# Attention's two score passes in 64-row tiles of the matmul array (one transformer layer, one core)

## The chip, the cores and the metric

One Trainium2 chip, one of its cores. The metric is the device time of one execution in microseconds (us); smaller is better. Engines are named as in the profile: PE (TensorE, matrix multiply; PEld is its weight load), DVE (VectorE), ACT (ScalarE), POOL (GpSimd), SP (SyncE, here the issuer of all DMAs).

## The reference, cut to what matters

Eight images of 1024 tokens, 128 channels. Everything is float32.

```python
h = x @ W + pos                                      # 29 features -> 128
h = h + attn(layernorm(h))                           # 8 heads of 16 channels, causal
h = h + ffn(layernorm(h))                            # shared swiglu + 8 experts, 2 of them per token
# attn:
scores = einsum('bhqd,bhkd->bhqk', Q, K)
attn = softmax((scores + mask) / math.sqrt(d), axis=-1)
out = einsum('bhqk,bhkd->bhqd', attn, V) @ Wo + bo
```

## The kernel before, in words

**Precision by stacking.** A head has only 16 channels. To keep float32 precision with the fast one-pass matmul type, Q and K are each split into a high and a low part, and three products (high x high, high x low, low x high) are stacked along the contraction rows: 3 x 16 = 48 rows. `k_stack` holds, for each of four head pairs, the even head's 48 rows from row 0 and the odd head's 48 rows from row 64. `q_stack` has a slot per head: an even head's rows are 0 to 47 and the rest of its slot is zero, an odd head's rows are 64 to 111 and rows 0 to 63 are zero. So one matmul over all rows picks the right head of the pair. The zeros are written once, at the start (`stacks_zeroed`: two memsets on DVE, one on POOL).

**Two score passes.** Pass 1 (`score`, line 494; 64 steps per image) computes scores with queries on the output partitions, rows 0 to 111 of the array; DVE adds the mask and takes the row maximum (`score`, line 747). A step of 128 queries has up to 1024 keys, so half the steps are one matmul and half are two: 96 matmuls of 256, 384 or 512 columns per image. Every 16 steps (a unit: four heads, half an image) `turn` transposes the maxima on PE (line 507), DVE splits them (lines 735, 737), and SP copies them as two rows (126 and 127) into `q_stack` (`maxima`, line 375: two DMAs per unit). Against them `k_stack` holds rows of -1. Pass 2 (`prob`, line 523; 96 matmuls per image) computes the scores again, keys on the output partitions, over all 128 rows, so that the maximum is already subtracted; ACT takes the exponential (line 975); `weigh` (line 542, 24 per image) multiplies with V: four heads side by side in four 32-column tiles of the array, as two halves of float32 each, 8 records. Both passes write two alternating buffers (banks `b4`, `b5` for `prob` and the narrow scores, `pair[0]`, `pair[1]` for the wide scores). Step p of `prob` waits for the exponential of step p - 2, and step s of `score` for the maximum of step s - 2.

**The order.** Each engine runs one list of stages, `PERIOD`, woven by hand from streams: s = pass 1, p = pass 2, w = weigh, m = the layer's middle and the next image's front (emb, turn1, q, k, v, and to, ant, oproj, z2t, gates, shared), f = the two matmul layers of the ffn (`in`, `expert`), c = combine. PE takes its list strictly in this order:

```python
WEAVE = (
    "ssppspspspsppswspsppsppwsppsppwsppspwpwsppsppwsspspwppsppspspwpspwpspsppwspspwpssppwppssppwppsps"
    "ppwppmpspwppmwppmppwppmppppwwppmwppmppmwppfpmfppfwpmpmmfpwpmfppfffppmwppfppmpwppppmwsswsswssmssf"
    "mcssfssmfcmfffmssfcmcmfmmssffsfmmfsfsmmfsffssfssfmssfssmccssfsfsfsfscc"
)
```

In a period pass 1 begins with the wide steps (score 32 to 63), and the narrow steps (0 to 31) of the next image end it. `FIRST` goes before the first period, `LAST_WEAVE` is the order of the last image. Six middle images run in a hardware loop.

**The stretches** of one period, in PE's order, from one stage to the next: A from score 32 to the first `to`; B from there to `k` of half 0; C to score 0; D to `emb` of half 1; E to `turn1` of half 1; F to `k` of half 1; G to the end. The stack copies of the next image's K and Q (`stacks`, line 367: twelve DMAs of 128 KB in row behind `k` of half 0) must land before score 0.

**Tiles of the array.** An instruction uses a tile of the array that covers its rows and columns. `weigh` is 128 rows x 32 columns; `emb` (line 437, 29 rows) and the bias matmul inside `shared` (line 644, 9 rows) are 32-row tiles; everything else is the whole 128 x 128.

Of the kernel before, what the change touches and what calls it, by code (L numbers as in the profile page):

```python
# [36 lines left out]
P = 128  # L37
# [5 lines left out]
G4 = 4  # L43
# [5 lines left out]


ODD = 64
STACK = ODD + 3 * DH
SHIFT = P - 2
EPS = 1e-5
MASK = -100000.0
VW = 32
# [108 lines left out]
def build(nc, x_t, tok_w, pos, wq, wk, wv, wo, bq, bk, bv, bo, ln_s, ln_b, w_in, w_shared, w_expert, w_bias,  # L165
          w_gate, b_gate, out):
    with ExitStack() as ctx:
# [3 lines left out]
        def sem(name):  # L171
            return ctx.enter_context(nc.semaphore(name))
# [36 lines left out]
        qk_h, qk_l = sb("qk_h", [P, 2, S], F32R), sb("qk_l", [P, 2, S], F32R)  # L209
        v = sb("v", [P, TILES, HEADS, VW])  # L210

        q_stack = sb("q_stack", [P, 2, HEADS, HALF], F32R)
        k_stack = sb("k_stack", [P, HEADS // 2, S], F32R)
        mx = sb("mx", [P, NS])
        mrow_h, mrow_l = sb("mrow_h", [UNIT_S, NU, P], F32R), sb("mrow_l", [UNIT_S, NU, P], F32R)
# [86 lines left out]
            sem(n) for n in ("ex_ready", "sela_made", "sel_made", "weighted", "ex_step"))  # L302
        out_done = [sem(f"out_done_{half}") for half in range(2)]
        zeroed, ident_made = sem("zeroed"), sem("ident_made")
        stacks_zeroed = sem("stacks_zeroed")
        went_on = sem("went_on")

        out_v = out.rearrange("b (t p) c -> b p t c", p=P)
# [28 lines left out]
        @block.sync  # L337
        def _(sp):
            def load_x(i):
                sp.dma_start(x_sb[:], x_t[:, bass.ds(i * S, S)]).then_inc(x_in, 16)  # L340

            load_x(0)
            for dst, src in ((tokw_sb, tok_w), (pos_sb, pos)):
                sp.dma_start(dst[:], src).then_inc(w_in0, 16)
            for dst, src in ((wq_sb, wq), (wk_sb, wk), (bq_sb, bq), (bk_sb, bk),
                             (wv_sb, wv), (bv_sb, bv), (bo_sb, bo)):
                sp.dma_start(dst[:], src).then_inc(w_in1, 16)
            for dst, src in ((wo_sb, wo), (lns_sb, ln_s), (lnb_sb, ln_b), (win_sb, w_in), (wshared_sb, w_shared),
                             (wex_sb, w_expert), (wbias_sb, w_bias), (wgate_sb, w_gate), (bgate_sb, b_gate)):
                sp.dma_start(dst if dst is win_sb or dst is wex_sb else dst[:], src).then_inc(w_in2, 16)  # L350

            sp.wait_ge(const_made, CONSTS)
            sp.wait_ge(stacks_zeroed, 3)
            for n in range(HEADS // 2):
                sp.dma_start(words(k_stack[SHIFT:P, n, :]), words(minus1.rearrange("r c n -> r (c n)"))).then_inc(ones_in, 16)

            def stacks(i, half, w):

                if w == 0:
                    sp.wait_ge(qkh_made, i * 4 + 2 * half + 2)  # L360
                    sp.wait_ge(qkl_made, i * 4 + 2 * half + 2)
                for n, part in enumerate((qk_h, (qk_h, qk_l)[w], (qk_l, qk_h)[w])):
                    for odd in range(2):
                        to = slice(odd * ODD + n * DH, odd * ODD + (n + 1) * DH)
                        stack = k_stack[to, :, halfs(half)] if w else q_stack[to, half, odd::2, :]
                        rows = part[odd * (P // 2):(odd + 1) * (P // 2), w, halfs(half)]
                        sp.dma_start(words(stack), words(rows)).then_inc(stack_in[half], 16)  # L367

            def maxima(i, u):

                g, half = UNITS[u]
                sp.wait_ge(ml_made, i * NU + u + 1)
                for row, part in ((SHIFT, mrow_h), (SHIFT + 1, mrow_l)):
                    dst = q_stack[row:row + 1, half, g * G4:(g + 1) * G4, :]
                    sp.dma_start(words(dst), words(part[:, u, :])).then_inc(m_in[u], 16)

            def store(i, half):
                sp.wait_ge(ex_step, (i * TILES + (half + 1) * HT) * COMBINE)
                sp.dma_start(out_v[i, :, tiles(half), :], acc[:, tiles(half), :]).then_inc(out_done[half], 16)

            def stage(i, st, loads=True):
                if st[0] == "turn":
                    maxima(i, st[1])
                elif st == ("k", 0):
                    stacks(i, 0, 0)
                    if not later(i):
                        stacks(i, 0, 1)
                elif st == ("k", 1):
                    stacks(i, 1, 0)
                    stacks(i, 1, 1)  # L390
                    if loads:
                        load_x(i + 1)
                elif st == ("combine", 3):
                    store(i, 0)
                elif st == ("combine", 7):
                    store(i, 1)

            def keys(i):

                sp.wait_ge(exp_done, i * NP_ * G4 + (KEYS_USED + 1) * G4)  # L400
                stacks(i + 1, 0, 1)

            def image(i, loads):
                for n, st in enumerate(PERIOD):
                    stage(i + of_next_image(st), st, loads)
                    if n == max(PERIOD.index(("k", 0)), PERIOD.index(("prob", KEYS_USED, G4 - 1))):
                        keys(i)

            for st in FIRST:
                stage(0, st)  # L410
            image(0, True)
            with sp.Fori(1, B - 2) as i:
                image(i, True)
            image(B - 2, False)
            for st in LAST:
                stage(B - 1, st)
            for half in range(2):
                sp.wait_ge(out_done[half], B * 16)
# [3 lines left out]
        def _(pe):  # L422
# [50 lines left out]
            def score(i, s):  # L473


                u, t, j = SCORE_STEPS[s]
                hd = UNITS[u][0] * G4 + j
                if s == 0:
                    pe.wait_ge(stack_in[0], i * 192 + 192)
                    if later(i):  # L480
                        pe.wait_ge(exp_done, i * NP_ * G4)
                if s == UNIT_S:
                    pe.wait_ge(ml_made, i * NU + 1)
                if s == 2 * UNIT_S:
                    pe.wait_ge(stack_in[1], i * 192 + 192)
                    if later(i):
                        pe.wait_ge(sel_made, i * TILES)
                if s >= 2:
                    pe.wait_ge(s_taken, i * NS + s - 1)
                n = (t + 1) * P  # L490
                dst = pair[s % 2] if t >= HT else (b4, b5)[s % 2]

                for a, b in ([(0, max(256, n))] if n <= HALF else [(0, HALF), (HALF, max(HALF + 256, n))]):
                    mm = nc.tensor.matmul(dst[:, a:b], q_stack[0:STACK, t // HT, hd, t % HT * P:(t % HT + 1) * P],  # L494
                                          k_stack[0:STACK, hd // 2, a:b], start=True, stop=True)
                mm.then_inc(s_ready, 1)

            def turn(i, u):
# [11 lines left out]
            def prob(i, k, j):  # L510

                u, kt = PROB_STEPS[k]
                g, half = UNITS[u]
                q0, c0 = prob_columns(k)
                if kt == 0 and j == 0:
                    pe.wait_ge(m_in[u], i * 32 + 32)
                if k == 0 and j == 0:
                    pe.wait_ge(ml_made, i * NU + 2)
                p = k * G4 + j
                if p >= 2:  # L520
                    pe.wait_ge(exp_done, i * NP_ * G4 + p - 1)
                hd = g * G4 + j
                nc.tensor.matmul((b4, b5)[p % 2][:, c0:HALF], k_stack[:, hd // 2, kt * P:(kt + 1) * P],  # L523
                                 q_stack[:, half, hd, c0:HALF], start=True, stop=True).then_inc(st_ready, 1)

            def weigh(i, k):

# [165 lines left out]
            pe.wait_ge(wsplit_qk, 4)  # L693
            for st in FIRST[1:]:
                stage(0, st)
            pe.wait_ge(ones_in, HEADS // 2 * 16)
            pe.wait_ge(w_in2, 9 * 16)
            pe.wait_ge(wsplit_h, 2)
            pe.wait_ge(wsplit_l, 2)
# [8 lines left out]
        def _(dve):  # L708
# [31 lines left out]
            def score(i, s):  # L740
                u, t, j = SCORE_STEPS[s]
                n = (t + 1) * P
                col = u * UNIT_S + j * HT + t % HT
                alone(dve, s_ready, i * NS + s + 1)
                src = (pair[s % 2] if t >= HT else (b4, b5)[s % 2])[:, 0:n]

                nc.vector.tensor_tensor_reduce(src, src, causal[:, S - n:S], 1.0, -3.0e38, ALU.add, ALU.max,  # L747
                                               mx[:, col:col + 1]).then_inc(s_taken, 1)
# [168 lines left out]
                for st in PERIOD:  # L917
                    stage(i + of_next_image(st), st)

            nc.vector.memset(words(k_stack[:, 0:2, :]), 0.0).then_inc(stacks_zeroed, 1)  # L920
            dve.wait_ge(w_in0, 2 * 16)
            stage(0, FIRST[0])
            dve.wait_ge(w_in1, 7 * 16)
# [4 lines left out]
                nc.vector.tensor_tensor(wqk_l[:, n, :], w[:], wqk_h[:, n, :].bitcast(F32),  # L928
                                        ALU.subtract).then_inc(wsplit_qk, 1)
            stage(0, FIRST[1])  # L930
            nc.vector.memset(words(k_stack[:, 2:, :]), 0.0).then_inc(stacks_zeroed, 1)
            dve.wait_ge(const_made, CONSTS)
            for st in FIRST[2:]:
                stage(0, st)
# [131 lines left out]
        def _(pool):  # L1066
# [2 lines left out]
            pool.wait_ge(zeroed, 1)  # L1069
            nc.gpsimd.affine_select(out=ident[:], in_=ident[:], compare_op=ALU.not_equal, fill=1.0, base=0,  # L1070
                                    pattern=[[-1, P]], channel_multiplier=1).then_inc(ident_made, 1)
            nc.gpsimd.memset(words(q_stack[:]), 0.0).then_inc(stacks_zeroed, 1)
            pool.wait_ge(const_made, 1)

            def constants():
# [171 lines left out]
```

## Time and profile before

| | us |
|---|---|
| time before, median of 3 runs (lowest, highest) | 1200.93 (1200.56, 1201.93) |
| span of the profiled execution, first to last instruction | 1198.4 |
| the median less this span (start and end around the program) | 2.5 |
| PE busy in the span | 1062.6 |
| DVE, ACT, POOL busy | 760.6, 629.2, 388.1 |

The profiled execution's time is its span with what lies around it; no time of its own is listed beside the three runs. A middle image takes 143.5 us. A matmul's busy time in the profile is its latency: it overlaps with the next one's, so the distance between two starts, not the duration, tells what an instruction costs PE.

### The profile page before, as it was taken

How to read it: one execution, taken by the hardware profiler on the slowest of the kernel's cores; microseconds unless marked ns; L12 is line 12 of the kernel's file. 1: busy time of each engine (PE TensorE's matmuls, PEld its weight loads, DVE VectorE, ACT ScalarE, POOL GpSimd, SP SyncE). 2: the span in 40 equal slices, each digit the busy share in tenths (PEclk: the TensorE clock that was granted, in tenths of full speed). 3: DMA queues.
4: the chain of work that ended last, by engine and by line, in shares of the span. 5: the costliest groups of instructions: out<-in, count | busy, mean ns of one | idle time of the engine just before them, and what ended most of it. 6: DMA issues, size and time to landing. Idle time of an engine off the chain costs nothing.

```text
span 1198.4 us, 20365 instructions
## 1 busy us (share of the span) xinstructions
PE 1062.6 (89%) x5632; PEld 707.3 (59%) x5632; DVE 760.6 (63%) x2118; ACT 629.2 (52%) x1395; POOL 388.1 (32%) x514
## 2 busy tenths in 40 slices
PE   2579988999799988899888998889989899899997
PEld 1345566556675566655666556755567455675575
DVE  3378547873768547686486854777467763778444
ACT  1226825567345745467344672546734576456744
POOL 5411424314341234313352142431433213341133
PEclk9969989999898998899889998989988999899999
DMA  3430033004040040400413003310314004040000
GB/s 94 71 40 2 14 41 59 19 2 54 10 59 10 1 53 10 67 1 1 53 26 50 1 11 42 55 22 1 41 12 66 13 2 53 10 63 1 1 2 18
DMA packets 28540, 34.39 MB, mean 29 GB/s; under 512 B 5402, under 2 KB 15552, under 8 KB 28336
## 3 DMA queue, kind: packets, MB, share of 16 engines
q1 hardware_dynamic: 28464, 33.55, 18.2%
q8 instruction: 26, 0.43, 0.1%
q14 instruction: 50, 0.41, 0.1%
HBM read 3.61 MB, written 4.19 MB: 7 GB/s over the span
## 4 chain that ended last, share of the span: by engine, by line
PE 62%; issue 11%; DVE 8%; DMA 6%; POOL 5%; SPq 4%; ACT 3%; DVEq 0%; POOLq 0%; ACTq 0%
PE bank L523 12%; PE pair L494 10%; PE bank L542 9%; PE bank L494 5%; DMA k_stack<-qk_h 5%; SPq L367 4%; PE pair L662 4%; PE pair L663 4%; PE pair L664 4%; PE bank L643 2%; ACT pt L975 2%; PE pair L425 1%; PE pair L426 1%; PE pair L427 1%; PE bank L644 1%
## 5 line engine op out<-in xcount | busy, mean ns | idle before, releaser
L975 ACT ACTIVATE pt<-bank 128x512 f32<-128x512 f32 (+3 forms) x768 | 348.6, 494 | 230.8 <-PE bank L523 223.6
L747 DVE CUSTOM_DVE_ANT_0 pair<-pair,causal 128x640 f32<-128x640 f32 (+3 forms) x256 | 258.8, 1046 | 59.3 <-PE pair L494 44.8
L523 PE MATMUL bank<-q_stack,k_stack 128*128 128x512 f32 (+2 forms) x768 | 268.9, 402 | 7.8 <-ACT pt L975 6.3
L523 PEld LDWEIGHTS bank<-q_stack,k_stack 128*128 128x128 f32 x768 | 137.9, 193 | 160.2 <-ACT pt L975 127.6
L1119 POOL TENSOR_SCALAR_AFFINE_SELECT pt<-pt 128x512 f32<-128x512 f32 x128 | 81.6, 638 | 391.9 <-ACT pt L975 391.9
L494 PE MATMUL pair<-k_stack,q_stack 112*128 112x512 f32 (+2 forms) x512 | 156.2, 396 | 22.6 <-DVE mx L747 12.3
L747 DVE CUSTOM_DVE_ANT_0 bank<-bank,causal 128x128 f32<-128x128 f32 (+3 forms) x256 | 122.6, 507 | 73.3 <-PE bank L494 73.1
L542 PE MATMUL bank<-pt,v 128*32 128x512 f32 (+3 forms) x1536 | 165.5, 503 | 2.2 <-POOL pt L1119 1.8
L494 PEld LDWEIGHTS pair<-k_stack,q_stack 112*128 112x128 f32 x512 | 90.9, 202 | 62.4 <-DVE mx L747 42.3
L494 PE MATMUL bank<-k_stack,q_stack 112*128 112x256 f32 (+2 forms) x256 | 90.0, 424 | 33.2 <-DMA k_stack<-qk_h 23.8
L662 PE MATMUL pair<-wex_h,hid_h 128*128 128x512 f32 x256 | 106.3, 415 | 0.7 <-POOL hid_l L1142 0.4
L663 PE MATMUL pair<-wex_l,hid_h 128*128 128x512 f32 x256 | 103.7, 405 | 0.0
L1021 ACT ACTIVATE from_act<-pair,gm 128x512 f32<-128x512 f32 x64 | 44.1, 689 | 113.3 <-PE pair L664 105.5
L664 PE MATMUL pair<-wex_h,hid_l 128*128 128x512 f32 x256 | 103.2, 403 | 0.0
L1150 POOL TENSOR_TENSOR from_dve<-from_act 128x256 f32<-128x256 f32 x64 | 46.7, 729 | 171.9 <-ACT from_act L1027 171.2
L1027 ACT ACTIVATE from_act<-from_dve,wsel 128x128 f32<-128x128 f32 x256 | 81.7, 391 | 37.6 <-DVE from_dve L899 37.6
L494 PEld LDWEIGHTS bank<-k_stack,q_stack 112*128 112x128 f32 x256 | 52.7, 227 | 54.5 <-DVE mx L747 20.0
L899 DVE SCALAR_TENSOR_TENSOR from_dve<-pair,gm,from_act 128x512 f32<-128x512 f32 x64 | 47.8, 746 | 41.8 <-PE pair L664 30.2
L747 DVE DVE_READ_ACCUMULATOR2_ANT mx<- 128x1 f32 x512 | 72.4, 141 | 0.1
L872 DVE SCALAR_TENSOR_TENSOR from_dve<-from_act,pair 128x512 f32<-128x512 f32 x64 | 43.9, 686 | 43.6 <-PE pair L427 33.3
L425 PE MATMUL pair<-z2t_h,win_h 128*128 128x512 f32 x128 | 58.1, 454 | 2.6 <-issue 1.8
L664 PEld LDWEIGHTS pair<-wex_h,hid_l 128*128 128x128 f32 x256 | 49.7, 194 | 12.4
(142 smaller groups left out, 1528.7 us busy)
## 6 DMA issues: line engine op xcount, KB each, us to landing
q_stack<-qk_h SPq DMA_DIRECT2D x64, 128.0 KB, 4.1
k_stack<-qk_h SPq DMA_DIRECT2D x64, 128.0 KB, 6.2
q_stack<-qk_l SPq DMA_DIRECT2D x32, 128.0 KB, 5.0
k_stack<-qk_l SPq DMA_DIRECT2D x32, 128.0 KB, 6.7
out<-h SPq DMA_DIRECT2D x16, 256.0 KB, 2.3
pt<-w_expert SPq DMA_DIRECT2D x1, 1024.0 KB
x_sb<-x_t SPq DMA_DIRECT2D x8, 116.0 KB
pos_sb<-pos SPq DMA_DIRECT2D x1, 512.0 KB
```

Of the source, the lines that this page charges most:

```text
L367: sp.dma_start(words(stack), words(rows)).then_inc(stack_in[half], 16)
L425: nc.tensor.matmul(dst, wh, xh, start=first, stop=False)
L494: mm = nc.tensor.matmul(dst[:, a:b], q_stack[0:STACK, t // HT, hd, t % HT * P:(t % HT + 1) * P], k_stack[0:STACK, hd // 2, a:b], start=Tru ...
L523: nc.tensor.matmul((b4, b5)[p % 2][:, c0:HALF], k_stack[:, hd // 2, kt * P:(kt + 1) * P], q_stack[:, half, hd, c0:HALF], start=True, stop= ...
L542: mm = nc.tensor.matmul(b6[32 * j:32 * j + VW, q0:HALF], v[:, kt, g * G4 + j, :], pt[:, k % PT_SLOTS, j, q0:HALF], start=(kt == 0), stop=( ...
L662: nc.tensor.matmul(dst, hid_h[:, c, tok], wex_h[:, c, w], start=(c == 0), stop=False)
L663: nc.tensor.matmul(dst, hid_h[:, c, tok], wex_l[:, c, w], start=False, stop=False)
L664: mm = nc.tensor.matmul(dst, hid_l[:, c, tok], wex_h[:, c, w], start=False, stop=(c == HID // P - 1))
L747: nc.vector.tensor_tensor_reduce(src, src, causal[:, S - n:S], 1.0, -3.0e38, ALU.add, ALU.max, mx[:, col:col + 1]).then_inc(s_taken, 1)
L975: nc.scalar.activation(pt[:, k % PT_SLOTS, j, q0:HALF], (b4, b5)[p % 2][:, q0:HALF], ACT.Exp, scale=0.25).then_inc(exp_done, 1)
L1027: nc.scalar.mul(from_act[:, t % 2, part], from_dve[:, t % 2, part], wsel[:, t, e:e + 1]).then_inc(weighted, 1)
L1119: nc.gpsimd.affine_select(out=d, in_=d, compare_op=ALU.is_ge, fill=0.0, base=0, pattern=[[0, G4], [1, P]], channel_multiplier=-1).then_inc ...
```

## The change

The zero rows go. `q_stack` gets one slot per head pair, like `k_stack`: an even head's rows 0 to 47 and its two rows of maxima at 48 and 49, an odd head's rows 64 to 111 and maxima at 112 and 113. Every matmul of both passes takes only its own head's rows, 0 to 47 or 64 to 111 in pass 1 and 0 to 49 or 64 to 113 in pass 2, so it runs in a 64-row tile of the array, the upper or the lower one. The memsets and their waits go. The maxima of a unit are sorted by even and odd heads (the column that a score step writes) and copied with four DMAs instead of two; the rows of -1 take eight DMAs instead of four. The order of the stages stays.

```diff
-STACK = ODD + 3 * DH
-SHIFT = P - 2
+STACK = 3 * DH
+SHIFTED = STACK + 2
-        q_stack = sb("q_stack", [P, 2, HEADS, HALF], F32R)
+        q_stack = sb("q_stack", [P, 2, HEADS // 2, HALF], F32R)
...
-            sp.wait_ge(stacks_zeroed, 3)
-            for n in range(HEADS // 2):
-                sp.dma_start(words(k_stack[SHIFT:P, n, :]), words(minus1.rearrange("r c n -> r (c n)"))).then_inc(ones_in, 16)
+            for odd in range(2):
+                for n in range(HEADS // 2):
+                    rows = slice(odd * ODD + STACK, odd * ODD + SHIFTED)
+                    sp.dma_start(words(k_stack[rows, n, :]),
+                                 words(minus1.rearrange("r c n -> r (c n)"))).then_inc(ones_in, 16)
...
-                        stack = k_stack[to, :, halfs(half)] if w else q_stack[to, half, odd::2, :]
+                        stack = k_stack[to, :, halfs(half)] if w else q_stack[to, half, :, :]
...
-                for row, part in ((SHIFT, mrow_h), (SHIFT + 1, mrow_l)):
-                    dst = q_stack[row:row + 1, half, g * G4:(g + 1) * G4, :]
-                    sp.dma_start(words(dst), words(part[:, u, :])).then_inc(m_in[u], 16)
+                for odd in range(2):
+                    for n, part in enumerate((mrow_h, mrow_l)):
+                        row = odd * ODD + STACK + n
+                        dst = q_stack[row:row + 1, half, g * 2:(g + 1) * 2, :]
+                        rows = part[odd * (UNIT_S // 2):(odd + 1) * (UNIT_S // 2), u, :]
+                        sp.dma_start(words(dst), words(rows)).then_inc(m_in[u], 16)
...
+                rows = slice(hd % 2 * ODD, hd % 2 * ODD + STACK)
...
-                    mm = nc.tensor.matmul(dst[:, a:b], q_stack[0:STACK, t // HT, hd, t % HT * P:(t % HT + 1) * P],
-                                          k_stack[0:STACK, hd // 2, a:b], start=True, stop=True)
+                    mm = nc.tensor.matmul(dst[:, a:b], q_stack[rows, t // HT, hd // 2, t % HT * P:(t % HT + 1) * P],
+                                          k_stack[rows, hd // 2, a:b], start=True, stop=True)
...
-                nc.tensor.matmul((b4, b5)[p % 2][:, c0:HALF], k_stack[:, hd // 2, kt * P:(kt + 1) * P],
-                                 q_stack[:, half, hd, c0:HALF], start=True, stop=True).then_inc(st_ready, 1)
+                rows = slice(hd % 2 * ODD, hd % 2 * ODD + SHIFTED)
+                nc.tensor.matmul((b4, b5)[p % 2][:, c0:HALF], k_stack[rows, hd // 2, kt * P:(kt + 1) * P],
+                                 q_stack[rows, half, hd // 2, c0:HALF], start=True, stop=True).then_inc(st_ready, 1)
...
-                col = u * UNIT_S + j * HT + t % HT
+                col = u * UNIT_S + (j % 2 * 2 + j // 2) * HT + t % HT
...
-            nc.vector.memset(words(k_stack[:, 0:2, :]), 0.0).then_inc(stacks_zeroed, 1)
-            nc.vector.memset(words(k_stack[:, 2:, :]), 0.0).then_inc(stacks_zeroed, 1)
-            nc.gpsimd.memset(words(q_stack[:]), 0.0).then_inc(stacks_zeroed, 1)
```

## Rows read from the trace of the kernel before

**Rows 1.** The page: busy time by engine, and the chain that ended last.

```profile
PE 1062.6 (89%) x5632; PEld 707.3 (59%) x5632; DVE 760.6 (63%) x2118; ACT 629.2 (52%) x1395; POOL 388.1 (32%) x514
PE 62%; issue 11%; DVE 8%; DMA 6%; POOL 5%; SPq 4%; ACT 3%; DVEq 0%; POOLq 0%; ACTq 0%
```

**Rows 2.** Windows: one image's stretches A, B, C, D, E, F+G, loop edge.

```profile
core 0: us, PE busy (x) PEld busy (x) DVE busy (x) ACT busy (x) POOL busy (x), PEclk, DMA share, GB/s
503.50:544.00 40.50, 39.18 (x210) 22.05 (x211) 33.92 (x66) 24.10 (x53) 5.72 (x9) 0.93 0.03 7
...
587.00:599.40 12.40, 12.06 (x59) 9.84 (x59) 8.34 (x33) 3.03 (x7) 1.66 (x3) 0.72 0.00 0
599.40:613.30 13.90, 9.83 (x51) 7.60 (x50) 11.18 (x41) 7.27 (x18) 8.67 (x14) 0.93 0.00 1
613.30:643.50 30.20, 29.28 (x136) 23.51 (x136) 21.96 (x64) 13.33 (x29) 11.63 (x13) 0.92 0.44 66
643.50:647.00 3.50, 1.37 (x6) 0.83 (x6) 0.53 (x2) 2.19 (x6) 2.56 (x6) 1.00 0.03 7
```

**Rows 3.** Timeline of PE, whole-array matmuls (start us, us of the group).

```profile
566.29 0.39 PE L425 MATMUL pair<-z2t_h,win_h 128*128 128x512 f32 x1
566.52 0.39 PE L426 MATMUL pair<-z2t_h,win_l 128*128 128x512 f32 x1
566.75 0.39 PE L427 MATMUL pair<-z2t_l,win_h 128*128 128x512 f32 x1
566.99 0.40 PE L523 MATMUL bank<-q_stack,k_stack 128*128 128x512 f32 x1
...
582.79 1.05 PE L468 MATMUL bank<-wv_sb,zt 128*128 128x128 f32 x8
```

**Rows 4.** Timeline of PE around one quad of 32-column tiles.

```profile
512.91 0.40 PE L523 MATMUL bank<-q_stack,k_stack 128*128 128x256 f32 x2
513.24 0.85 PE L542 MATMUL bank<-pt,v 128*32 128x384 f32 x8
514.02 0.68 PE L494 MATMUL pair<-k_stack,q_stack 112*128 112x512 f32 x2
514.53 0.40 PE L523 MATMUL bank<-q_stack,k_stack 128*128 128x256 f32 x2
```

**Rows 5.** Timeline of PE, 128-row and 9-row matmuls in turn.

```profile
206.25 0.48 PE L644 MATMUL bank<-wbias_sb,cnt_t 9*128 9x128 f32 x2
206.67 0.71 PE L643 MATMUL bank<-wshared_sb,hid 128*128 128x128 f32 x4
207.31 0.48 PE L644 MATMUL bank<-wbias_sb,cnt_t 9*128 9x128 f32 x2
```

**Rows 6.** Groups of PE by shape (busy us, mean ns of one | idle before).

```profile
L523 PE MATMUL bank<-q_stack,k_stack 128*128 128x512 f32 x384 | 157.7, 455 | 4.9 <-ACT pt L975 4.2
L542 PE MATMUL bank<-pt,v 128*32 128x512 f32 x768 | 102.3, 605 | 0.0
```

**Rows 7.** Waits (us in total, times, longest us).

```profile
PE bank L446 <- DVE z L723: 34.1, 9, 7.0
PE bank L494 <- DMA k_stack<-qk_h: 23.8, 8, 6.0
```

**Rows 8.** Timeline at the start of the program: memsets, -1 rows, first stack copies.

```profile
1.53 6.92 POOL L1072 MEMSET q_stack<- 128x8192 f32 x1
15.05 0.24 POOL L1095 TENSOR_SCALAR var<-mv 128x4 f32<-128x4 f32 x1 [6.60 <-issue]
...
21.72 2.55 SPq L355 DMA_DIRECT2D k_stack<-hid_l  x4
32.08 1.31 SPq L367 DMA_DIRECT2D q_stack<-qk_h  x2
```

**Rows 9.** Copies of the maxima: SP's issues, time to landing, the matmul behind.

```profile
523.41 0.51 SPq L375 DMA_DIRECT2D q_stack<-mrow_h  x1
523.97 0.58 SPq L375 DMA_DIRECT2D q_stack<-mrow_l  x1
...
q_stack<-mrow_l SPq DMA_DIRECT2D x32, 8.0 KB, 1.9
...
527.64 0.50 PE L523 MATMUL bank<-q_stack,k_stack 128*128 128x512 f32 x1
```

**Rows 10.** Timeline of PE in a stretch at a lower granted clock.

```profile
615.48 0.63 PE L426 MATMUL pair<-z2t_h,win_l 128*128 128x512 f32 x1
615.90 0.63 PE L427 MATMUL pair<-z2t_l,win_h 128*128 128x512 f32 x1
```

More of the change, by code:

```diff
@@ L304, in build @@
         zeroed, ident_made = sem("zeroed"), sem("ident_made")
-        stacks_zeroed = sem("stacks_zeroed")
         went_on = sem("went_on")
@@ L515, in prob @@
                 if kt == 0 and j == 0:
-                    pe.wait_ge(m_in[u], i * 32 + 32)
+                    pe.wait_ge(m_in[u], i * 64 + 64)
                 if k == 0 and j == 0:
@@ L695, in _ @@
                 stage(0, st)
-            pe.wait_ge(ones_in, HEADS // 2 * 16)
+            pe.wait_ge(ones_in, HEADS * 16)
             pe.wait_ge(w_in2, 9 * 16)
```

## Prediction

> **What bounds the kernel now.** I read the page first: PE is busy 89% of the span, DVE 63%, ACT 52%, and 62% of the chain that ended last is PE [rows 1]. Busy time of PE is latency, so the second view is the table of windows over one image of 143.5 us [rows 2]: the reader is to look for stretches in which PE has nearly no gap. Those are A (39.18 of 40.50 us), D, and F with G (29.28 of 30.20). DVE is the next engine in A, 33.92 of 40.50 us, 84%. In E PE has gaps of 4 us, and at the loop edge all engines stand still. The waits name what PE stands for: the z of the next layernorm, 34.1 us in all, and the stack copies, 23.8 us in 8 waits, the longest 6.0, so 2.5 us in each of the others, just ahead of score 0 [rows 7]. Nowhere does a long wait of PE on ACT appear. So what counts in A, B, D, F and G is the time that PE's ordered list takes, and this change touches only that list.
>
> **The price of a matmul.** In an unbroken stream the starts of 512-column matmuls are 0.23 us apart and those of 128-column ones (1.05 us for 8, the last 0.27 long) 0.11 us [rows 3]; I take 0.175 and 0.117 us for 384 and 256 columns, in proportion. The number of rows does not enter: the 48 or 50 rows stream as long as the 112 or 128. So the change gains nothing on a matmul alone. It can gain only where an even and an odd head stand side by side and run at the same time.
>
> **Do two tiles run at the same time?** The trace has this for column tiles: a 512-column instruction of `weigh` lasts 605 ns, but the group's 768 cover only 102.3 us, 133 ns each [rows 6], and eight of 384 columns are through in 0.85 us [rows 4], while eight one after another would take 8 x 0.175 = 1.4. No row tile stands beside another in this trace, so the gain has the bounds nothing and the whole shorter matmul of each pair. I take that they overlap, since the column tiles do. The Trainium skill, "TensorE: Matmul & The Clock Gate", section on packing small matmuls, says that matmuls in different row groups start some 4 ns apart and gives 3.07 times for four row tiles; by it the whole shorter matmul would be hidden, my upper bound.
>
> **What a change of tile costs.** This is the other side. From a whole-array stream into the quad: two 256-column matmuls at 512.91, the quad at 513.24, 0.33 us for 0.23 of stream: 0.10 more. After it: 512 and 384 columns from 514.02 to 514.53, 0.51 us for 0.41: again 0.10 more [rows 4]. The 9-row tile shows the same for rows: from 206.25 to 207.31 is 1.06 us for six matmuls of 128 columns, which stream in 0.67; two changes cost 0.39, 0.19 each [rows 5]. So each change of tile shape, in either direction, costs PE about 0.19 us when PE is streaming: a part before it (the array runs empty) and a part after it (the weight load lies open). The first matmul behind a wait already has its load open, so there the price is less; for the mean I take 0.17. Bounds: 0.10 (one part only) and 0.19. The Trainium skill, "TensorEngine Tiling (Array Packing)", Key Properties, says that changing the tiling mode drains the engine. By the trace the drain is only half: a reload of the weights comes behind it.
>
> **How many changes are new.** `weigh` breaks the stream with and without the change. New are those where a score or prob step stands beside a whole-array stage. Counted along `PERIOD`: A 2 (one `turn`), B 17, C 8, D 7, E 2, F 6, G 17. Islands of one or two steps between f and m stages are the reason. `LAST` has 2 in its A and 26 behind.
>
> **What of them is hidden.** C's 8 cost 1.4 us ahead of score 0, where PE waits 2.5 us for copies that were set off by `k` [rows 7]: hidden, 0 (bare: 1.4 per image). E's 2 end in the wait for z: hidden. The other 47 and A's 2, 49 x 0.17 = 8.3 us per image, lie on PE's path.
>
> **What the pairs give back outside A.** In B, D, F and G stand 26 neighbouring steps of different halves; hiding the shorter of each, in order, makes 3.9 us if the second is always ready. The second p waits for the exponential of two steps before, and a wide share of ACT's time is taken. I take 0.6 of it: 2.3 us. Bounds 0 and 3.9.
>
> **Stretch A.** 43 neighbours of different halves; hiding the shorter ones makes 6.2 us of PE. But DVE has 33.92 us of work there, so A can't fall by more than 6.6, and each step waits for the buffer of two before: DVE or ACT will end more of the waits. I take half, 3.0 us. Against this, the maxima: unit 2's were issued at 523.41 and 523.97, land 1.9 us after the second or a little more, and its first prob starts at 527.64 [rows 9], with some 1 to 1.5 us to spare. Two more issues of 0.5 to 0.6 us take 1.1 us of this, and A's shorter list the rest: a new stall of about 0.5 us. Nothing else is queued behind them on SP there. The other units' copies have a stage or more to spare. A gains 2.5 us. Bounds 0 and 5.
>
> **The start.** POOL's memset ends at 8.45 and POOL then stands until 15.05 for another reason. SP issues the -1 rows at 21.72, 2.55 us for four; eight take 5.1, until about 27, and the next DMAs can't go before 32.08 [rows 8]. DVE's memsets lie in its idle time. Zero; if the copies were earlier, 2.6 us of SP would show. `FIRST` has six new changes beside waits for DVE: zero.
>
> **The sum.** A middle period: 8.3 - 2.3 - 2.5 = +3.5 us, seven times +24.5. The last image: 28 x 0.17 = 4.8, less 2.5 and 1.7, +0.6. Together +25: span 1198.4 to 1223.5, with the 2.5 us around it 1226. The median of the runs, 1200.93, is this span and those 2.5 us, so it moves by the same 25 us, 2.1%.
>
> **The rivals.**
> *No overlap.* The two row tiles run one after the other, so the change does not do what it is for. For it: no row here shows two row tiles together. Against it: the column tiles. Then per period 8.3, last image 4.8: +63, time 1264; at 0.19 a change, +70, 1271.
> *A change costs the drain only* (faster). If the upper and lower row tile take their weights while the other works, the second part of the price goes: 0.10 each, 4.9 per period. 4.9 - 3.9 - 2.5, with the pairs then always ready, is -1.5; seven times and the last image (2.8 - 2.5 - 2.5 = -2.2) make -13: 1188. It decides from about 0.10 to 0.13 us a change: at 4.8 us given back, 4.8 / 49 = 0.10 with my halves, 0.13 with full pairs outside A. For it: the first part alone is all that a drain takes. Against it: [rows 5] is a row tile, and paid both. By the skill's sentence on the drain alone, this is the case that it would make.
> *The clock.* Granted clock is 0.72 in D and 0.92 in F and G, and matmuls of 512 columns then start 0.42 us apart [rows 2, 10], the 1.2 GHz level against 2.4. It fell after PE had waited. 0.72 over D's 12.40 us means about 7 us at the low level. PE with more holes may spend half as much again there in each image, 3.5 us at half speed: a loss of 1.7 us, eight times 14, on top of the forecast: 1240. If half an array counted as idle, all of A would run at the low level, and 20 us per image would be lost; A's present mix of tiles at 0.93 speaks against it.
>
> **Chances.** Forecast 0.52, no overlap 0.16, drain only (or A gaining nearly all that DVE leaves) 0.20, clock 0.12. The predicted time is that of the first, 1226. Its own range, from the bounds of price and pairs, is 1205 to 1245. The range for all reaches to 1190 below and to 1268 above. What a measurement here can tell from no change is about 0.2%, 2.4 us. Faster 0.21, within 0.05, slower 0.74.
>
> **What would show it.** Right: pairs of lines 494 and 523 that start under 0.02 us apart; a first matmul behind each island 0.1 us late and the one behind it another 0.1; D, F and G longer by 1 to 3 us; A shorter by 1 to 4 with DVE near 90%; the wait for the stack copies shorter. Wrong: 0.23 us between the starts of a ready pair; islands in G that cost under 0.1 per side; a granted clock in A below 0.9; A no shorter.

## The result, and the profile after

The changed kernel takes 1366.0 us (median of 4 runs, 1353.6 to 1380.2) against 1200.7: 13.4% slower, ratio 1.134, 95% interval 1.129 to 1.139. Forecast were 1226 and at most 1268. The profiled execution took 1365.2 us, its span 1363.3. (Runs over 1.5% above the fastest of the same kernel count in its median but not in its ratio: 1380.2 here, and in the experiments one of four with all heads in one tile, two of four on 80 rows and one of four with tiles in A only.)

The page of the changed kernel: busy time by engine, the granted clock of TensorE in 40 slices (tenths of full speed), and the chain.

```profile
PE 1216.7 (89%) x5632; PEld 699.1 (51%) x5632; DVE 758.6 (56%) x2116; ACT 633.5 (46%) x1395; POOL 380.4 (28%) x513
...
PEclk9856799577895899866988599966988589885799
...
PE 65%; issue 12%; DVE 7%; POOL 5%; DMA 4%; SPq 4%; ACT 3%; DVEq 0%; POOLq 0%; ACTq 0%
```

Against [rows 1] the other engines do the same work; only PE's grew, and its share of the chain. The clock has slices at 5 or 6, near half speed, in every period. The windows say in which stretch: here A of one image (from its first wide score to its first `to`), first of the kernel before with the pause at the loop edge, then of the changed one. The columns are those of [rows 2]; the granted clock stands third from the end.

```profile
500.00:544.00 44.00, 40.60 (x216) 22.96 (x217) 34.26 (x68) 26.37 (x59) 8.36 (x15) 0.92 0.03 7
```

```profile
567.00:623.20 56.20, 51.20 (x215) 23.56 (x212) 34.19 (x67) 25.76 (x57) 7.76 (x13) 0.59 0.02 6
```

The reader is to see three things: 12 us more, DVE's and ACT's work unchanged, and a granted clock of 0.59 where it was 0.92. It has two levels, 1.2 and 2.4 GHz, so 0.59 means that 82% of this stretch ran at the low one. That is where more than half of the time went. Averaged over the six middle images, from the first wide score to the first `to` and so on (us per image, in brackets the part at the low clock):

| | A, with the loop edge | B and C | D to G |
|---|---|---|---|
| before | 42.8 (4.5) | 43.4 (1.3) | 56.4 (11.9) |
| changed | 54.2 (42.9) | 47.5 (7.7) | 61.2 (12.0) |

The tile changes came out as worked out. The timeline of PE in the changed kernel, in G at the high clock:

```profile
715.03 0.39 PE L670 MATMUL pair<-wex_h,hid_l 128*128 128x512 f32 x1
715.35 0.39 PE L499 MATMUL bank<-k_stack,q_stack 48*128 48x256 f32 x2
715.66 0.50 PE L668 MATMUL pair<-wex_h,hid_h 128*128 128x512 f32 x1
716.00 0.40 PE L669 MATMUL pair<-wex_l,hid_h 128*128 128x512 f32 x1
```

The group at 715.35 holds two matmuls of 256 columns, one per tile, and lasts 0.39 us in all, as long as one: they run together. From the matmul before the island to the island 0.32 us pass for 0.23 of stream, from it to the next 0.31 for 0.12 (the two overlap), and 0.34 for 0.23 to the one behind: 0.97 us where a whole-array stream takes 0.70. The price is 0.39, of which the overlap gives back 0.12.

Of the waits that hid something, the one for the stack copies shrank and the one for z stayed, to compare with [rows 7]:

```profile
PE bank L450 <- DVE z L729: 34.1, 9, 7.0
...
PE bank L499 <- DMA k_stack<-qk_h: 17.5, 8, 6.0
```

### The profile page after: what moved, and what is told of

Read it like the earlier page. It is cut to its first block, busy times and chain, and to the rows that moved or that the text cites. A ratio compares the mean times of both kernels' runs of the same rounds, so it can differ in the third digit from the quotient of the medians.

```text
span 1363.3 us, 20429 instructions
## 1 busy us (share of the span) xinstructions
PE 1216.7 (89%) x5632; PEld 699.1 (51%) x5632; DVE 758.6 (56%) x2116; ACT 633.5 (46%) x1395; POOL 380.4 (28%) x513
## 4 chain that ended last, share of the span: by engine, by line
PE 65%; issue 12%; DVE 7%; POOL 5%; DMA 4%; SPq 4%; ACT 3%; DVEq 0%; POOLq 0%; ACTq 0%
PE bank L529 13%; PE bank L548 11%; PE pair L499 9%; PE bank L499 5%; PE pair L668 4%; DMA k_stack<-qk_h 4%; SPq L368 4%; PE pair L669 3%; PE pair L670 3%; ACT pt L979 2%; PE pair L429 2%; PE bank L649 2%; PE pair L430 1%; PE pair L431 1%; PE bank L650 1%
## 5 line engine op out<-in xcount | busy, mean ns | idle before, releaser
L529 PE MATMUL bank<-q_stack,k_stack 50*128 50x512 f32 (+2 forms) x768 | 310.5, 539 | 23.8 <-ACT pt L979 22.6
L529 PEld LDWEIGHTS bank<-q_stack,k_stack 50*128 50x128 f32 x768 | 145.5, 237 | 237.2 <-ACT pt L979 153.5
L548 PE MATMUL bank<-pt,v 128*32 128x512 f32 (+3 forms) x1536 | 221.8, 660 | 1.1 <-POOL pt L1122 0.2
L499 PE MATMUL pair<-k_stack,q_stack 48*128 48x512 f32 (+2 forms) x512 | 192.5, 565 | 25.4 <-DVE mx L753 15.9
L499 PEld LDWEIGHTS pair<-k_stack,q_stack 48*128 48x128 f32 x512 | 104.7, 287 | 75.4 <-DVE mx L753 50.4
L668 PE MATMUL pair<-wex_h,hid_h 128*128 128x512 f32 x256 | 115.8, 452 | 0.4 <-POOL hid_l L1145 0.4
L499 PE MATMUL bank<-k_stack,q_stack 48*128 48x256 f32 (+2 forms) x256 | 83.4, 490 | 27.5 <-DMA k_stack<-qk_h 17.5
L499 PEld LDWEIGHTS bank<-k_stack,q_stack 48*128 48x128 f32 x256 | 38.1, 211 | 78.9 <-issue 35.9
L429 PE MATMUL pair<-z2t_h,win_h 128*128 128x512 f32 x128 | 64.5, 504 | 1.7 <-issue 0.7
L668 PEld LDWEIGHTS pair<-wex_h,hid_h 128*128 128x128 f32 x256 | 50.3, 196 | 26.1 <-issue 14.8
```

What stands on the lines that cost most here:

```text
L429: nc.tensor.matmul(dst, wh, xh, start=first, stop=False)
L499: mm = nc.tensor.matmul(dst[:, a:b], q_stack[rows, t // HT, hd // 2, t % HT * P:(t % HT + 1) * P], k_stack[rows, hd // 2, a:b], start=True ...
L529: nc.tensor.matmul((b4, b5)[p % 2][:, c0:HALF], k_stack[rows, hd // 2, kt * P:(kt + 1) * P], q_stack[rows, half, hd // 2, c0:HALF], start= ...
L548: mm = nc.tensor.matmul(b6[32 * j:32 * j + VW, q0:HALF], v[:, kt, g * G4 + j, :], pt[:, k % PT_SLOTS, j, q0:HALF], start=(kt == 0), stop=( ...
L668: nc.tensor.matmul(dst, hid_h[:, c, tok], wex_h[:, c, w], start=(c == 0), stop=False)
```

## The experiments

Two theories at the outset. **Active rows**: the granted clock follows how many rows of the array work, and how much of the time; a 48-row matmul counts for less than one on 112 or 128. **Holes**: the pairs leave PE idle more, and the clock falls for that. A third view is that the clock is a side matter and tile changes cost more than thought.

### Streams on PE alone

Behind the last image of the kernel before, PE runs streams of 512-column matmuls and nothing else:

```diff
+            stream(0, 112, 150)
+            stream(0, 48, 150)
+            stream(0, 112, 100)
+            pairs(48, 150)
+            stream(0, 112, 100)
+            stream(0, 80, 150)
+            stream(0, 112, 100)
+            for _ in range(40):
+                pairs(48, 1)
+                stream(0, 112, 3)
...
+            pairs(64, 150)
```

> The kernel before, with matmul streams of PE alone appended behind the last image (they write spare PSUM and change no output; about 560 us more at the high clock). 512-column matmuls in order: 150 on 112 rows (whole array), 150 in the lower 64-row tile (48 rows), then, always behind 100 on 112 rows: 150 pairs lower and upper tile (48 rows each), 150 on 80 rows (whole array), 40 times one pair and three on 112 rows, 40 quads of 32-column tiles in float32, 150 pairs on 64 rows each. Theory rows (the chip grants the low clock when only part of the array's rows works): the stream in one tile falls to granted clock 0.5, matmuls 0.43 us apart; pairs use 96 rows and stay high or fall late; 80 rows lies between. Theory holes (it grants the low clock in stretch A because pairs leave PE idle more): no stream without holes falls, all at 1.0 and 0.23 us apart. Both: starts of a pair under 0.02 us apart; one pair and three matmuls take 0.23 x 4 plus 2 x 0.19 = 1.3 us.

The windows of this run: 112 rows, the lower tile alone, 112 rows behind it (first at the low clock, then high), pairs on 48 rows, 80 rows, pair and three in turn, `weigh`'s 32-column tiles four at a time on 128 rows, pairs on 64 rows. Columns: us, then PE's busy time, PEld, DVE, ACT, POOL, granted clock.

```profile
1205.00:1233.00 28.00, 28.00 (x125) 23.20 (x124) 0.00 (x0) 0.00 (x0) 0.00 (x0) 1.00 0.00 1
...
1236.80:1295.00 58.20, 58.20 (x138) 44.46 (x136) 0.00 (x0) 0.00 (x0) 0.00 (x0) 0.50 0.00 0
1295.20:1301.70 6.50, 6.50 (x16) 5.11 (x16) 0.00 (x0) 0.00 (x0) 0.00 (x0) 0.50 0.00 0
1301.70:1320.80 19.10, 19.10 (x86) 15.77 (x85) 0.00 (x0) 0.00 (x0) 0.00 (x0) 1.00 0.00 1
1321.10:1355.20 34.10, 34.10 (x301) 28.03 (x300) 0.00 (x0) 0.00 (x0) 0.00 (x0) 1.00 0.00 1
1378.20:1412.10 33.90, 33.90 (x151) 28.07 (x150) 0.00 (x0) 0.00 (x0) 0.00 (x0) 1.00 0.00 0
1434.90:1487.70 52.80, 52.80 (x199) 26.41 (x198) 0.00 (x0) 0.00 (x0) 0.00 (x0) 1.00 0.00 0
1511.30:1545.60 34.30, 34.30 (x321) 10.29 (x320) 0.00 (x0) 0.00 (x0) 0.00 (x0) 1.00 0.01 1
1568.70:1602.80 34.10, 34.10 (x301) 27.98 (x300) 0.00 (x0) 0.00 (x0) 0.00 (x0) 1.00 0.00 1
```

PE was busy without a gap in every one of them, and in the lower tile alone (48 rows) it was put to 0.50, 58.2 us for 138 matmuls, 0.42 each, until whole-array matmuls had run for a while. Holes can't do that. Pairs stayed at 1.00 and took 34.1 us for 300 matmuls, 0.114 us each: the overlap is complete. 80 rows without a gap stayed at 1.00 too, and so did the 32-column tiles. The Trainium skill ("TensorE: Matmul & The Clock Gate", Part 1) has the clock follow how busy PE has been; by that alone the gapless stream in one tile would have stayed high. The measurement decides: how much of the array is in use counts too. And the timeline of the island part:

```profile
1440.34 0.50 PE L717 MATMUL bank<-k_stack 48*128 48x512 f32 x2
1440.78 0.98 PE L710 MATMUL bank<-k_stack 112*128 112x512 f32 x3
1441.68 0.50 PE L717 MATMUL bank<-k_stack 48*128 48x512 f32 x2
```

1.34 us for a pair and three, against 4 x 0.227 = 0.91 of stream (the overlap counted): 0.21 a change. The price from [rows 4, 5] was 0.19.

### All heads in one tile

```diff
-                rows = slice(hd % 2 * ODD, hd % 2 * ODD + STACK)
+                rows = slice(0, STACK)
...
-                rows = slice(hd % 2 * ODD, hd % 2 * ODD + SHIFTED)
+                rows = slice(0, SHIFTED)
```

> The changed kernel, but all heads in the lower tile, so that nothing overlaps (the odd heads' scores are computed from the even heads' rows). Theory rows: granted clock in stretch A as low as in the changed kernel (about 0.6) or lower, and time above it, 1400 us or more. Theory holes: PE streams as many columns in A as before, the clock there stays near 1.0, and the time is before plus the tile changes alone, 1265 to 1275 us.

1525 us, ratio 1.270 (1.266 to 1.273); A takes 65.0 us, 61.2 of them at the low clock. PE has as many columns to stream as before and nothing runs side by side, so it has fewer holes than in the changed kernel (in A of one image it is busy for 62.4 of 65.2 us, against 51.2 of 56.2), and the clock is still lower. Theory holes is out, and it is seen that the pairs, costly as they are, keep the clock better than one tile does.

### Fewer rows without tiles

No tile, no pairs, no new tile change: the kernel before, both passes on rows 0 to 95, 0 to 79, 0 to 65 of the whole array.

```diff
-                    mm = nc.tensor.matmul(dst[:, a:b], q_stack[0:STACK, t // HT, hd, t % HT * P:(t % HT + 1) * P],
-                                          k_stack[0:STACK, hd // 2, a:b], start=True, stop=True)
+                    mm = nc.tensor.matmul(dst[:, a:b], q_stack[0:80, t // HT, hd, t % HT * P:(t % HT + 1) * P],
+                                          k_stack[0:80, hd // 2, a:b], start=True, stop=True)
```

(and the same range in `prob`)

> The kernel before, whole-array tile, but both score passes take rows 0 to 79 only instead of 112 and 128 (the scores of odd heads and the subtraction of the maximum are left out). No tile change is added and nothing overlaps. Theory rows, if active rows count: clock in A under 0.9 and time 1210 to 1300 us. If the tile's shape counts or theory holes: same as before, 1201 us, clock 0.94.

> The kernel before, whole-array tile, both score passes on rows 0 to 95 (part of the odd heads' scores and the subtraction of the maximum are left out). Theory active rows: between the kernel before (112 and 128 rows, 1199 us, 4.5 us per image of stretch A at the low clock) and the run on 80 rows (1313 us, 36 us): 1215 to 1280 us. A rival with a sharp edge between 80 and 112: either end, 1199 or 1310.

> As the run before it, on rows 0 to 65, so nearly the rows of one 64-row tile but with no tile change and no pairs. Theory active rows: A almost wholly at the low clock, 1340 to 1420 us. If what counts is the 64-row tile itself: as on 80 rows, 1313 us.

| rows (pass 1 / pass 2) | time, us | ratio (95%) | A (low clock), us |
|---|---|---|---|
| 112 / 128, before | 1200 | | 42.8 (4.5) |
| 96 / 96 | 1220.1 | 1.016 (1.015 to 1.018) | 44.9 (9.7) |
| 80 / 80 | 1313.4 | 1.086 (1.082 to 1.091) | 53.5 (36.3) |
| 66 / 66 | 1386.9 | 1.157 (1.152 to 1.162) | 62.1 (56.5) |

The windows of A in one image on 96 and on 66 rows; the reader is to look at the clock, third from the end:

```profile
507.80:553.20 45.40, 42.25 (x215) 23.55 (x216) 34.37 (x68) 26.34 (x58) 8.30 (x15) 0.89 0.02 7
```

```profile
562.10:627.30 65.20, 62.39 (x215) 35.82 (x216) 35.48 (x68) 26.48 (x59) 8.37 (x15) 0.52 0.02 5
```

This is the decisive series. The same instructions in the same order, only with fewer active rows, lose up to 16%. (The four executions on 80 rows scatter from 1298 to 1340 us; A's figures are of one at 1318.) On 80 rows the gapless stream above stayed high while A falls, so rows alone don't decide it. That the gaps between A's matmuls make the difference is likely; no run varied them alone. From this series an image's A lengthens by (62.1 - 42.8) / (56.5 - 4.5) = 0.37 us for each us at the low clock.

### Tiles, but all their rows

Maxima in rows 62, 63 and 126, 127, zero rows in between, so that a tile has 62 or 64 active rows. Order, pairs and tile changes stay as in the changed kernel.

```diff
-STACK = 3 * DH
+STACK = 62
 SHIFTED = STACK + 2
```

> The changed kernel with the maxima moved to rows 62, 63 and 126, 127 and zero rows in between, so that pass 1 takes 62 rows of its tile and pass 2 all 64 instead of 48 and 50. Order, tiles, pairs and waits (but for the zeroing at the start) as in the changed kernel. Theory active rows (the granted clock follows how many rows of the array work and how much of the time): more rows at the same schedule, so the low-clock time in A shrinks; 1230 to 1320 us, clock 0.84 to 0.93. Rival, the tile's shape alone: as the changed kernel, 1350 to 1380 us, clock 0.81.

1305.3 us, ratio 1.085 (1.081 to 1.090): 61 us come back from zeros. A takes 48.4 us (24.4 low). At the same tile shape, order and tile changes, the rows alone move the clock. The kernel is still 105 us slower than the one before: it keeps the tile changes, and a step that runs without a partner still uses half the array.

### Tiles in stretch A only

```diff
+                rows = slice(hd % 2 * ODD, hd % 2 * ODD + SHIFT) if t >= HT else slice(0, P - 2)
...
+                rows = slice(hd % 2 * ODD, hd % 2 * ODD + ODD) if k < 14 else slice(0, P)
```

> Tiles of 62 and 64 rows for the steps of stretch A alone (wide scores, and pass 2 up to its 56th step), whole-array matmuls on zero rows elsewhere (126 and 128 rows; the narrow scores of even heads there take in the maxima of the image before, so those scores are off). The tile changes of B to G are gone and the pairs of A stay. Theory active rows: if 62 and 64 rows keep the clock in A mostly high, A shortens by 2 to 4 us per image: 1170 to 1195 us; if not, A runs at the low clock for part of the time: 1200 to 1260 us. If tile changes were the main cause of the loss, not the clock: below 1200 in either case.

1246.8 us, ratio 1.035 (1.033 to 1.037), with A at 47.5 us (22.6 low) and the other stretches nearly as before (44.0 and 56.9). With nearly all tile changes outside A gone, the kernel is still 3.5% slower, and 4.7 of the 5.7 us that a middle image is longer lie in A, where 18 us more are at the low clock.

### Tiles in D to G only

```diff
+                rows = slice(hd % 2 * ODD, hd % 2 * ODD + 3 * DH) if t < HT else slice(0, STACK)
```

> The kernel before with its zero rows, but the narrow steps of pass 1 (score 0 to 31, which stand in stretches D to G) in 64-row tiles; the wide steps and pass 2 use the whole array. Adds some 31 tile changes per middle image and none in A, B and C. At 0.17 to 0.19 us each, less 1 to 1.7 us of overlap: +25 to +35 us, 1226 to 1236, with the clock in A unchanged. If the clock falls wherever tiles stand among other work: D to G at 0.5, +60 us or more.

1229.0 us, ratio 1.024 (1.022 to 1.027), A at 43.2 (4.6), D to G 60.0 against 56.4. So +29 us for the narrow scores' tile changes, with no loss of clock: inside what was expected. The low clock takes 10.2 us of D to G, 11.9 before, so tiles of 48 rows that stand among whole-array matmuls did not lower it.

### More rows where there were few

Pass 1 on 126 rows instead of 112; and, apart from it, the token matmul and the bias matmul of `shared` on 128 rows (with zero rows) instead of 29 and 9, which takes 160 tile changes out of the kernel before.

```diff
-                    mm = nc.tensor.matmul(dst[:, a:b], q_stack[0:STACK, t // HT, hd, t % HT * P:(t % HT + 1) * P],
-                                          k_stack[0:STACK, hd // 2, a:b], start=True, stop=True)
+                    mm = nc.tensor.matmul(dst[:, a:b], q_stack[0:SHIFT, t // HT, hd, t % HT * P:(t % HT + 1) * P],
+                                          k_stack[0:SHIFT, hd // 2, a:b], start=True, stop=True)
```

```diff
-        cnt_t = sb("cnt_t", [EXPERTS + 1, HALF])
+        cnt_t = sb("cnt_t", [P, HALF])
...
+            for tile in (x_sb, tokw_sb, wbias_sb, cnt_t):
+                nc.vector.memset(tile[:], 0.0).then_inc(padded, 1)
```

> The kernel before, pass 1 on rows 0 to 125 instead of 0 to 111 (the added rows are zero), nothing else. Theory active rows: 149 us of the span before are at the low clock; some of it goes, mostly near the scores: 1180 to 1198 us. Rival, active rows matter only far below the whole array: no change, 1198 to 1202.

> The kernel before, with zero rows added to the token matmul (29 rows) and the bias matmul of shared (9 rows), so that both run on the whole array: 2 x 16 and 8 x 16 tile changes go, 160 in all. At 0.19 us each 30 us, some of it ahead of waits: 1170 to 1182 us, and less if the fuller rows also shorten the low-clock time. If a tile change costs its drain only: 1185.

> The kernel before with pass 1 on 126 rows and the token and bias matmuls on the whole array: the two edits that cost nothing or gained, together. 1186 to 1190 us: the tile changes that went, no more from the rows of pass 1. If more active rows near the edge help once the small tiles are gone: under 1182.

Pass 1 on 126 rows: 1199.4 us, ratio 1.000 (0.999 to 1.001), no change; a miss. With pass 1 at 112 rows there is nothing left to gain. Without the small tiles: 1188.0 us, ratio 0.990 (0.988 to 0.992). The timeline of `shared` in that run, to compare with [rows 5]:

```profile
205.26 0.61 PE L649 MATMUL bank<-wshared_sb,hid 128*128 128x128 f32 x4
205.71 0.39 PE L650 MATMUL bank<-wbias_sb,cnt_t 128*128 128x128 f32 x2
205.93 0.61 PE L649 MATMUL bank<-wshared_sb,hid 128*128 128x128 f32 x4
```

Six matmuls now take 0.67 us, not 1.06: a `shared` stage saves 1.2 us (3.50 to 2.34 from its first to its last 128-row matmul), 16 of them 19. The total fell by 11 only, and I had written 18 to 30. The span's time at the low clock rose from 147 to 166 us in the same run; why it rose was not tried. At the 0.33 to 0.37 us lost for each (see below), these 19 us would be 6 to 7 of the 8 us that are missing, an estimate. Both edits together: 1186.5 us, ratio 0.989 (0.987 to 0.990), the fastest kernel of this study, 1.1% below the kernel before and 13% below the changed one.

## Why the prediction was wrong

**The step that failed** is the clock, under the rivals: "If half an array counted as idle, all of A would run at the low level, and 20 us per image would be lost; A's present mix of tiles at 0.93 speaks against it." The mechanism was named, and its place too. For an A wholly at the low level 20 us was even the right size: on 66 rows of the whole array, with 56.5 of 62.1 us low, A got 19.3 us longer. In the changed kernel, with its pairs, A got 11.4 us longer with 38.4 us more at the low clock. What was wrong is the evidence that I set against it. The 32-column tiles of `weigh` are four at a time on all 128 rows, so they use the whole array (a stream of them alone stayed at 1.00) and say nothing of a part of it. In the sum the clock stood at nothing, and the rival that I priced had only 14 us for it, for D and not for A.

**Its size.** A: 38.4 us more at the low clock. Between this kernel and the one with tiles in A only, (54.2 - 47.5) / (42.9 - 22.6) = 0.33 us are lost for each; the rows series gives 0.37; the prediction priced it at 0.5. So, by estimate, the clock cost A some 13 to 14 us per image, and B and C, with 6.4 us more at the low level, 2. Eight images make 120 to 130 of the 165 us lost. The remaining 35 to 45 are what the forecast's own terms were about, and they stood at 25: outside A they cost 4.8 and 2.0 us per image, where 5.7 was forecast, and A gave back 1.3 to 2.8 where 2.5 was (see below).

**Point by point.**
- PE's list bounds A, B, D, F, G: it fits. DVE's and ACT's work did not change, and PE's share of the chain rose.
- A matmul costs its columns, not its rows: right for the stream at a given clock, wrong as the whole truth, since the rows in use move the clock.
- Two row tiles overlap fully: right (0.114 us a matmul in pairs). The rival of no overlap is out.
- 0.17 to 0.19 us a tile change, half drain and half reload: right (0.39 for two in the island above, 0.21 each in the stream). The rival of drain only is out. The Trainium skill's drain ("TensorEngine Tiling (Array Packing)", Key Properties) is borne out, and it is about half of what one pays: behind the island above, the matmul after the first is 0.11 us late as well.
- D to G: the 30 changes of D, F, G at 0.17 make 5.1 us per image, less about 1 of the 2.3 us that the pairs were to give back outside A; measured 4.8 at an unchanged clock, and 3.6 in the kernel that tiles only there. B and C: 17 changes, 2.9 us, less the rest of the 2.3, so 1.6; measured 4.1, about 2.0 without the clock. Right.
- The gain of A, 2.5 us: open. Taken back to the 4.5 us of low clock of before, A of the changed kernel comes to 54.2 - 0.33 x 38.4 = 41.5 us, against 42.8, a gain of 1.3; at 0.37 for each us it comes to 40.0, a gain of 2.8. Both are extrapolations; no run had pairs in A at the high clock throughout.
- The maxima: their four issues now stand 0.68 us apart instead of two 0.56 apart, and in one image the first prob of unit 2 starts at 600.91, 2.5 us after the last issue at 598.37. But it starts 0.31 us behind the last matmul of `weigh` in this image and three others, as in the kernel before (527.33 to 527.64), and 0.56 us in the four where the clock was low there. The new stall of 0.5 us did not show.
- The wait for the stack copies took up tile changes: right in kind, 23.8 us before and 17.5 after.
- The start: right, score 0 begins at 46.9 us against 46.8.

## What to carry to other kernels

At a given clock a matmul on few rows costs as much time as one on 128, and where such matmuls make up most of a stretch with gaps, as in A, they let the clock fall for all that stands around them (in D to G they did not). So zero rows can be worth keeping: here, filling the tiles with zeros gave back 61 us, and cutting the rows of an untouched schedule to 66 cost 187. Before tiling an array in a kernel with gaps, ask of each stretch how much of the array will be at work at once, and look for a stretch or write a stream that shows the clock at just that. A change of tile shape costs about 0.2 us on this PE stream, so islands of one or two tiled steps don't pay here, and padding the odd 9- or 29-row matmul to the whole array gained 1%.

## What the runs showed of the hardware

- A gapless stream of 512-column matmuls on 48 rows is held at the 1.2 GHz level (0.50 for 58 us), while 80 rows, or two tiles of 48 side by side, stay at 2.4 GHz.
- In a stretch of the kernel the effect is graded by active rows: 4.5, 9.7, 36.3 and 56.5 us of an image's A at the low clock for 112/128, 96, 80 and 66 rows. In D to G, narrow scores on 48 rows among whole-array matmuls left it as it was (10.2 us against 11.9). Rows of zeros count as active: `q_stack`'s idle half was zero all along, and zeros in rows 48 to 61 of each tile brought 61 us back.
- Two 64-row tiles run fully together, 0.114 us per 512-column matmul against 0.227, with float32 of the one-pass type.
- A change of tile shape costs 0.19 to 0.21 us in a stream at the high clock, about half of it ahead of the next matmul and half behind it.
- From one run to the next the time of the kernels with more low clock scatters more: 1354 to 1380 us for the changed kernel and 1298 to 1340 on 80 rows, against 1198 to 1202 for the one before.
